# Reordered taps, points, final scaling and rounding in tile 0, an earlier split in tile 1, and four own buffers for the unit turns

## The reference

```python
x = x + _L0_conv_ref(_gn(x), ...)   # depthwise convs, sampled values, attention
x = x + _L1_conv_ref(_gn(x), ...)   # token attention with a wide MLP beside it
```

## Time and profile before

| what | value |
| --- | --- |
| runs | 2822.07, 2825.60, 2829.56 us (median 2825.60) |
| profiled execution, own time | 2823.88 us |
| its span | 2822.1 us |
| TensorE busy | 96% |
| VectorE busy | 70% |
| ScalarE busy | 42% |
| GpSimd busy | 23% |
| mean granted TensorE clock | 0.967 of full |

### The profile page before, as it was taken

The page is one execution under the profiler, slowest core; times in us unless marked ns, Lnnn a source line. Parts: engine busy times, 40 slices in busy tenths (PEclk is TensorE's granted clock), DMA queues, the critical chain, the costliest instruction groups (busy, mean ns, idle before and its releaser), DMA issues.

```text
span 2822.1 us, 40251 instructions
## 1 busy us (share of the span) xinstructions
PE 2697.0 (96%) x14382; PEld 2447.3 (87%) x14382; DVE 1981.0 (70%) x2513; ACT 1176.4 (42%) x2039; POOL 658.5 (23%) x219
## 2 busy tenths in 40 slices
PE   6998799999999999999999999999999999999999
PEld 4556798899998899899998899899999899999998
DVE  5988785888887684988886674888887634434443
ACT  3432465444342465444432265444443254333332
POOL 0020142222222043222224033322224033211220
PEclk9998899999999999999999999999999999999999
DMA  5257632343338632333446743233436832112110
GB/s 222 58 156 258 216 96 81 102 110 113 103 101 255 219 123 82 101 101 101 107 120 200 261 129 100 70 103 110 122 101 178 281 110 79 43 43 52 47 43 30
DMA packets 208431, 347.62 MB, mean 123 GB/s; under 512 B 24288, under 2 KB 191840, under 8 KB 205408
## 3 DMA queue, kind: packets, MB, share of 16 engines
q1 hardware_dynamic: 182192, 311.60, 34.0%
q10 hardware_dynamic: 21552, 14.05, 3.7%
q0 software_dynamic: 4480, 19.27, 2.4%
HBM read 241.31 MB, written 103.56 MB: 122 GB/s over the span
## 4 chain that ended last, share of the span: by engine, by line
PE 71%; issue 10%; DMA 8%; DVE 6%; ACT 3%; POOL 2%; SPq 1%; ACTq 0%; DVEq 0%; POOLq 0%
PE bank L781 15%; PE bank L782 15%; PE bank L783 15%; PE bank L827 3%; PE bank L986 3%; PE bank L988 3%; PE bank L987 3%; PE bank L1177 3%; PE bank L1009 3%; PE bank L1163 2%; DVE AC L2391 2%; DMA r_scr<-rr 2%; POOL rq L701 1%; DMA X<-x_scr 1%; PE bank L1121 1%
## 5 line engine op out<-in xcount | busy, mean ns | idle before, releaser
L1751 ACT ACTIVATE S<-bank,b1p 128x448 f32<-128x448 f32 x336 | 212.4, 632 | 836.6 <-PE bank L783 795.1
L2391 DVE SCALAR_TENSOR_TENSOR AC<-XV,wfold,AC 128x1568 f32<-128x1568 f32 x288 | 530.0, 1846 | 2.8
L781 PE MATMUL bank<-SH,W2H 128*128 128x448 f32 x1008 | 391.3, 388 | 7.8 <-DVE SL L2360 7.7
L781 PE MATMUL bank<-XRH,W1H 128*128 128x448 f32 x1008 | 378.7, 376 | 0.7 <-ACT S L1751 0.7
L783 PE MATMUL bank<-SH,W2L 128*128 128x448 f32 x1008 | 375.9, 373 | 0.0
L782 PE MATMUL bank<-SL,W2H 128*128 128x448 f32 x1008 | 375.7, 373 | 0.0
L782 PE MATMUL bank<-XRL,W1H 128*128 128x448 f32 x1008 | 374.3, 371 | 0.0
L783 PE MATMUL bank<-XRH,W1L 128*128 128x448 f32 x1008 | 372.6, 370 | 0.0
L701 POOL TENSOR_TENSOR rq<-qn,nhalf 112x32 f32<-112x32 f32 x28 | 181.9, 6496 | 465.7 <-DVE qn L2330 465.7
L2360 DVE TENSOR_TENSOR SL<-S,SH 128x448 fp32r<-128x448 f32 x336 | 207.2, 618 | 92.4 <-ACT SH L1754 91.5
L705 POOL TENSOR_TENSOR ro<-on,nhalf 112x32 f32<-112x32 f32 x28 | 180.1, 6434 | 299.5 <-DVE on L2351 299.4
(11 more groups left out here) (228 smaller groups left out, 5171.9 us busy)
## 6 DMA issues: line engine op xcount, KB each, us to landing
XV<-in_xp SPq DMA_DIRECT2D x36, 870.0 KB, 7.3
XC<-in_xp SPq DMA_DIRECT2D x14, 1682.0 KB, 9.9
CQ<-q_scr SPq DMA_DIRECT2D x28, 672.0 KB, 7.1
CX<-in_x SPq DMA_DIRECT2D x28, 672.0 KB, 4.9
x_scr<-CX SPq DMA_DIRECT2D x28, 672.0 KB, 5.3
X<-x_scr SPq DMA_DIRECT2D x28, 672.0 KB, 4.2
V<-v_scr SPq DMA_DIRECT2D x28, 672.0 KB, 7.0
Y<-x_scr SPq DMA_DIRECT2D x28, 672.0 KB
```

Source lines behind the costliest of these rows:

```text
L781: mm(o, wh, xh, start=first, stop=False)
L1751: fn(S[:, j % 2, :], bank[j % 2][:, 0:T], ACT.Silu, bias=b1p[:, j:j + 1]).then_inc(s["s_s"], 1)
L2391: stt(o, XV[h][:, ky:ky + HR, kx:kx + W], wfold[:, kind, k, 3 * ky + kx:3 * ky + kx + 1], o, ALU.mult, ALU.add).then_inc(s["va"], 1)
```

## The change

All edits are in the passes with a next image, in tiles 0 to 3.

- VectorE, tile 0: the taps per place are 0, 1, 1, 1, 2, 2, 2, 2, 2, 2, 1 instead of 0, 0, 0, 1, 2, 2, 2, 2, 2, 2, 3. The first stands before the copy of the offsets, the second before the first `o_scale`. `o_final` moves from behind the sixth split to ahead of the two taps before it; `attended_l` moves ahead of the seventh split; the sixth group of taps moves behind `scale_x` and ahead of `query_norm`. `sampling_points` moves from tile 1 to tile 0, behind the eighth split.
- VectorE, tile 1: the first split stands ahead of the first tap.
- ScalarE, tile 0: `unit_start(0, 0)` stands before `norm_in`; `attended_h` and the tanh stand behind the last `query_out` and ahead of `roots_spread` and `silu(n, 7)`. They stood behind `silu(n, 7)` and at the tile's end.
- Unit turns: groups of 4, 4, 4 and 2 in the same banks 6, 7, 5, 6, with four buffers and four store semaphores instead of three. VT3 lies behind RB, in the room that the sampling stage uses as VS.

(The count of splits starts at 0.)

```diff
+VU = (4, 4, 4, 2)
+VU0 = (0, 4, 8, 12)
...
-        VT2 = sb("VT2", [TS, VG[2] * P], at=at)
-        VT = (VT0, VT1, VT2, VT0)
+        VT2 = sb("VT2", [TS, VU[2] * P], at=at)
...
+        VT3 = sb("VT3", [TS, VU[3] * P], at=[at[0] + T * 4])
+        VT = (VT0, VT1, VT2, VT3)
...
-    VST = (HEAD + 192, HEAD + 112, HEAD + 64)
+    VST = (HEAD + 192, HEAD + 112, HEAD + 64, HEAD)
...
-                    act.wait_ge(s[f"pair_st{i % 3}"], VST[i % 3] + (b * (2 * KC) + c) * (32, 16, 16)[i % 3] + i // 3 * 16)
-                    fn(VT[i][:, 0:VG[i] * P], bank[(6, 7, 5, 6)[i]][0:TS, 0:VG[i] * P], ACT.Copy).then_inc(s["vt_ev"], 1)
+                    act.wait_ge(s[f"pair_st{i}"], VST[i] + (b * (2 * KC) + c) * 16)
+                    fn(VT[i][:, :], bank[(6, 7, 5, 6)[i]][0:TS, 0:VU[i] * P], ACT.Copy).then_inc(s["vt_ev"], 1)
...
                 def tile(n, t):
                     first, last = t == 0, t == STRIPS - 1
                     before = nxt and 1 <= t <= KC
                     silu(n, 0)
                     silu(n, 1)
+                    if nxt and first:
+                        unit_start(0, 0)
                     if not last:
                         norm_in(b * KVX + KVT + t + 1)
                     silu(n, 2)
-                    if nxt and first:
-                        unit_start(0, 0)
                     if before:
                         for i in range(3):
                             unit_out(t - 1, 1, i)
...
                         roots_out(n + 1)
                         query_out(n + 1, 1)
                         query_out(n + 1, 2)
+                        if first:
+                            attended_h(n, first)
+                            if nxt:
+                                tanh(b + 1)
                         roots_spread(n + 1)
                     silu(n, 7)
-                    if not last:
+                    if not first and not last:
                         attended_h(n, first)
                     for j in range(8, JC - 1):
                         silu(n, j)
...
                 alone(act)
                 for t in range(STRIPS - 1):
                     tile(n0 + t, t)
-                    if nxt and t == 0:
-                        tanh(b + 1)
                 if nxt:
                     last_tile(n0 + STRIPS - 1, b + 1)
                 else:
...
                         stt(Y[:, k, :], bank[2 + k][:, 0:T], bo[:, k:k + 1], Y[:, k, :], ALU.add, ALU.add).then_inc(s["y_s"], 1)
 
                 AT = (1, 1, 1, 2, 2, 2, 2, 2, 1, 1, 1)
-                AT0 = (0, 0, 0, 1, 2, 2, 2, 2, 2, 2, 3)
+                AT0 = (0, 1, 1, 1, 2, 2, 2, 2, 2, 2, 1)
 
                 def conv(t, part):
 
...
                     first, last = t == 0, t == STRIPS - 1
                     if not first:
                         output(n - 1)
-                    conv(t, 0)
-                    split_s(n, 0)
+                    if t == 1:
+                        split_s(n, 0)
+                        conv(t, 0)
+                    else:
+                        conv(t, 0)
+                        split_s(n, 0)
                     if nxt and t >= 1:
                         strip_stats(b + 2, t - 1, X0Q)
                     if first:
                         state_heads()
+                        conv(t, 1)
                         if nxt:
                             dve.wait_ge(s["dots"], HEAD + b + 2)
                             cp(OFF[:, :, :].rearrange("p t a -> p (t a)"), bank[7][0:TK, 0:2 * STRIPS]).then_inc(s["off_put"], 1)
                             sampling_offsets(b + 1)
-                    if nxt and t == 1:
-                        sampling_points(b + 1)
-                    conv(t, 1)
+                    if not first:
+                        conv(t, 1)
                     split_s(n, 1)
                     if first:
+                        conv(t, 2)
                         o_scale(n, 0)
                         o_scale(n, 1)
-                    conv(t, 2)
+                    else:
+                        conv(t, 2)
                     if last:
                         o_final(n)
                     else:
...
                         o_norm(n)
                     conv(t, 4)
                     split_s(n, 5)
+                    if first:
+                        o_final(n)
                     conv(t, 5)
                     split_s(n, 6)
-                    if first:
-                        o_final(n)
-                    elif not last:
+                    if not last:
                         attended_l(n)
-                    conv(t, 6)
+                    if not first:
+                        conv(t, 6)
                     split_s(n, 7)
-                    if first:
-                        attended_l(n)
                     if not last:
                         scale_x(n + 1)
+                    if first:
+                        conv(t, 6)
+                    if not last:
                         query_norm(n + 1, 7)
                     conv(t, 7)
                     split_s(n, 8)
+                    if nxt and first:
+                        sampling_points(b + 1)
                     if not last:
                         o_scale(n + 1, 0)
                         o_scale(n + 1, 1)
```

More of the change, by code:

```diff
@@ L201, in build @@
         at[0] = xrr_end
[L202 removed]
+        VT1 = sb("VT1", [TS, VU[1] * P], at=at)
         CQ0 = sb("CQ0", [P, KC, T], at=list(at))
@@ L274, in build @@
             f1 s_s sh sl f2 mh ml pj y_s""".split()
-        names += ["gtp", "oc_ev", "pair_st2"] + [f"gath{t}" for t in range(GR)]
+        names += ["gtp", "oc_ev", "pair_st2", "pair_st3"] + [f"gath{t}" for t in range(GR)]
         s = {n: sem("s_" + n) for n in names}
@@ L290, in build @@
         ahead = """otp ktp oa ka kt_ev kt_st dots off_put va qa vtp vt_ev pair_st0 pair_st1
-            at_mm k_red k_hat v1_st0 v1_st1 k_ev v_ev s_s sl f2 pair_st2 y_s y_st""".split()
+            at_mm k_red k_hat v1_st0 v1_st1 k_ev v_ev s_s sl f2 pair_st2 pair_st3 y_s y_st""".split()
         block = ctx.enter_context(nc.Block())
@@ L553, in store_unit @@
                         c = conv_unit(t, h)
-                        for i in range(len(VG)):
-                            r0 = (h * HT + VG0[i]) * TS
+                        for i in range(len(VU)):
+                            r0 = (h * HT + VU0[i]) * TS
                             sp.wait_ge(s["vt_ev"], VTT + b * (KC * 8) + c * 4 + i + 1)
-                            sp.dma_start(pair_d[r0:r0 + VG[i] * TS, t * P:(t + 1) * P].rearrange("(s p) c -> p s c", p=TS),
-                                         VT[i][:, 0:VG[i] * P].rearrange("p (s c) -> p s c", c=P)).then_inc(s[f"pair_st{i % 3}"], 16)
+                            sp.dma_start(pair_d[r0:r0 + VU[i] * TS, t * P:(t + 1) * P].rearrange("(s p) c -> p s c", p=TS),
+                                         VT[i][:, :].rearrange("p (s c) -> p s c", c=P)).then_inc(s[f"pair_st{i}"], 16)
                     else:
@@ L726, in image @@
                 if nxt:
-                    pool.wait_ge(s["pair_st0"], VST[0] + (b + 1) * (KC * 64))
-                    pool.wait_ge(s["pair_st1"], VST[1] + (b + 1) * (KC * 32))
-                    pool.wait_ge(s["pair_st2"], VST[2] + (b + 1) * (KC * 32))
+                    for i in range(len(VU)):
+                        pool.wait_ge(s[f"pair_st{i}"], VST[i] + (b + 1) * (KC * 32))
                     pool.wait_ge(s["va"], taps_done(b, CV - 1, 0))
@@ L1219, in turn_unit @@
                         pe.wait_ge(s["vt_ev"], VTT + b * (KC * 8) + c * 4 + 1)
-                    for j in range(VG[i]):
-                        last = tr(bank[VTB[i]][0:TS, j * P:(j + 1) * P], AC[h][:, (VG0[i] + j) * TS:(VG0[i] + j + 1) * TS], ident[:, :])
+                    for j in range(VU[i]):
+                        last = tr(bank[VTB[i]][0:TS, j * P:(j + 1) * P], AC[h][:, (VU0[i] + j) * TS:(VU0[i] + j + 1) * TS], ident[:, :])
                     last.then_inc(s["vtp"], 1)
```

2 lines of the change are left out of this document (1 added, 1 removed).

## The result

The changed kernel took 2795.78 us in the median of 6 runs (2790.73 to 2804.53), the kernel before 2823.84: a ratio of 0.9914 [0.989, 0.9938]. One of the six executions of the kernel before took 5983.52 us; it is not in the ratio, and without it the median is 2822.07. So the changed kernel is 26 to 28 us faster by the medians, 0.9% by the ratio; 2815.5 was forecast, with 2808 to 2822 as the range, so the time lies outside it, on the fast side. Measured again, beside the first experiments, it took 2811.83 us (2804.57 to 2818.14, 10 runs) against 2826.08: 0.9946 [0.9927, 0.9964], 14 us. The granted clock of those ten runs was 0.965 to 0.970, that of the first six 0.966 to 0.974. So part of the first gain is clock that these six runs had and the ten had not. Both gains are more than the 8.5 us of my sum: the upper bound of the second interval, 0.9964, is still 10 us.

A forecast was written before the change was run, and what follows sets the result against it. TensorE, busy 2697.0 of 2822.1 us, was taken as the bound. Gains of 3.9 + 8.5 + 4.7 = 17.1 us less 3.5 + 4.2 + 0.9 = 8.6 gave 8.5 us: 2815.5 us forecast, range 2808 to 2822.

The forecast's parts named there:

- my sum: Whole change: removed TensorE waits gain 17.1 us, 8.6 us are given back, leaving 8.5 us.
- The waits named: TensorE's waits: V's 3.4 us and SL's 7.7 go, VT's 5.0 fall to about 0.7, ML's 0.79 stays.
- the two causes given for SL: Tile 1: fewer taps behind the last root and first split ahead of the tap; all five SL waits go, 8.5 us.
- The 0.9 us for X's load: Tile 2's X load shares queues with the output's store: 0.3 us per pass, 0.9 us given back.
- Fourth attend, 3.5 + 3R = 7.7 us given back: Tile 0: the later query root makes TensorE's fourth attend wait 1.1 + R us in each of three passes.
- R: Tile 0: how much later RB's load lands than VectorE wants it; taken as 1.4 us, bounds 0 and 2.5.
- rival (a): Tile 0: RB is as quick as before, R = 0; gain 12.7 us, 2811 us; chance 0.20.
- net nothing, at most 5 us either way: Half clock behind long waits: three such waits removed, three of 2.6 us brought; at most 3 x 1.7 us.
- Rival (d): Clock: half-clock stretches behind long waits cost 1.7 us each, net nothing; no chance of its own given.
- tile 0's order: Tile 0 as a whole loses: 3.9 us gained from V's wait, 7.7 given back at the fourth attend.
- the own buffers: Unit turns: each of six VT waits shrinks by at most 0.8 us, 4.7 us gained in all.
- turned against the change (2819): Idle-gap rule: new, longer waits could each bring a half-clock stretch, 3.4 us more, 2819 us.

The follow-up runs named there:

- the first experiments: The changed kernel again, and with shared buffer, tile 1's order or tile 0's order put back; ratios to the kernel before 0.9946, 0.9978, 0.994, 0.9909.
- the first kernel with spread norms: The changed kernel with the norm products spread, a quarter ahead of fc2(6) and one behind each of its three outputs; 2791.34 us, ratio to before 0.9892.
- the wide base: The changed kernel with norm products spread wider, to the last two thirds of fc1(9), and the fourth attend one step later; 2775.36 us, again 2771.06 (0.9842, 0.9839).

## Why the prediction was wrong

- **The waits named were the right ones.** V 3.4, SL 7.7 and VT 4.4 of 5.0 us went, and ML stayed, as the steps had it. Of the two causes given for SL, the taps were enough; once they are moved, the split ahead of the tap and the points moved out of tile 1 add nothing that the runs show. The 0.9 us for X's load doesn't show either: in tile 1 ScalarE waited 2.23, 0.32 and 0.54 us for it, against 1.54, 1.67 and 1.75 before, and the only wait of TensorE for VT that is left is 0.6 us.
- **Fourth attend, 3.5 + 3R = 7.7 us given back: this term failed too.** The mechanism is right, its size was too large, and the clock hid it. RB was issued 1.5 us after the turn of V began, not 2.2 (489.05 and 487.58), and it had landed when the scaling of X started at 493.95, 4.9 us later:

```profile
489.05 0.35 ACTq L1629 DMA_DIRECT2D RB<-r_scr  x1
```
```profile
493.95 1.56 DVE L2303 TENSOR_TENSOR X<-X,RB 128x1344 f32<-128x1344 f32 x1 [0.29 <-DMA RB<-r_scr]
...
498.95 0.18 DVE L2334 COPY qn<-bank 112x32 f32<-112x32 f32 x1
...
506.24 1.02 DVE L2345 TENSOR_TENSOR QQ<-bank,rq 112x384 f32<-112x384 f32 x2 [0.60 <-POOL rq L704]
```

  VectorE waited 0.29 us for it: R is 0.3, not 1.4, close to the 0 of rival (a), and the wait would have been 1.4 us a pass, 4.4 in all (the first kernel with spread norms shows 1.24, 1.33 and 1.38). V's load was issued at 488.95, just ahead of RB, and landed after 5.8 us, later than RB after 4.9. So RB didn't queue behind V; it took 1.5 us more than the 3.4 of this place before. The Trainium skill, "DMA: Bandwidth & Descriptors", section "Queues, rings and completion order", says that each DMA engine alternates between the queues that have work; the trace agrees, with RB's 4.9 us inside the 3.4 to 6.3 of the earlier trace rows and its landing ahead of V's.
- **The clock, "net nothing, at most 5 us either way": this is the step that failed.** Rival (d) took one fall after one of three waits as chance and looked at no other. Many falls are tied to places, behind the norm block (17 of its 24 places before) and behind long waits, and the change moves them. In its profile the new fall in tile 0 costs 8.5 us and all other half clock is 15.5 us less, so half clock costs 88 us where it cost 95: 7 us gained, not nothing. Of the 25.5 us between the two profiles, 18.5 are left for idle time; 16.2 of them are my gains with X's load taken off and without the attend, 17.1 - 0.9. The single terms point the same way: tile 0's order loses 8.0 us where the sum had 3.8, the own buffers gain 6.6 where it had 4.7, and the taps 11.6 where it had 8.5. Each of these alone is within the spread of the runs from the sum; on the wide base, where the waits are longer too, the taps' 16.7 and the buffers' 12.8 are clear of it. In the second measurement the clock does come to about nothing, with means of 0.967 after and 0.968 before, as (d) had it, but as a balance of larger parts: the 14 us there are near 16.2, with the fall in tile 0 in the place of the attend's wait and about as much clock gained elsewhere. That the forecast was nearer to this measurement is luck in so far as these parts cancel. In the first measurement the mean clock was 0.970, and 0.003 of 2800 us are 8 us more, over half of the 14 by which the two measurements differ.
- **The rule on idle gaps** (the Trainium skill, "TensorE: Matmul & The Clock Gate", section "Why this matters for your kernels", says that idle gaps between bursts of matmuls cost throughput by the clock) was weighed in the prediction for waits alone and turned against the change (2819). Where the waits are several us, the trace agrees (5.41 us idle, 0.54 granted). For the most frequent falls no idle gap is needed: in tile 1 of the kernel before TensorE was busy 3.20 of 3.20 us ahead of the fall. There the measurement decides: the clock fell with no idle gap, behind the block of eight-column products, and in the ten profiles with that block spread it fell behind it in 1 of 240 places.
- **The range** was built from R and the buffers and gave the clock 1.7 us steps; it should have had the run to run spread of the clock (0.965 to 0.970 over ten runs of one kernel, some 14 us) and what the change does to the falls.

Open is why tile 0's block loses the clock in all three passes in one order and in none in the other, with the same instructions and starts a microsecond or so apart: no run changed that start alone. Open is also what set the higher clock of the first six runs, and how much of the 15.5 us of clock gained outside tile 0 is the change's doing: one profile of the kernel before is all there is to compare with, and part of the difference lies in stages that the change doesn't touch.

## What to carry to other kernels

Before the waits of a tuned kernel whose TensorE is busy 96% are summed, list the stretches at half clock and look what stands ahead of each. A block of narrow products that costs 2.4 us by its own time cost up to 3.4 us more behind it, and in the changed kernel spreading it between wide products, with its consumer one step later, gave more than the whole change: from 0.9946 to 0.9842 [0.9814, 0.987] of the kernel before. It is no gain by itself everywhere: in the kernel before, the same edit gave only 0.9959 [0.9945, 0.9973], since a wait on VectorE grew to 5.6 us; the wait and the block had to go together. An instruction moved ahead on an engine that works in order helps its consumer only if what then stands between the two is no longer than before; count both sides of the move.

## What was not expected of the hardware

The clock fell behind 2.4 us of products of 8 columns with TensorE busy throughout, and didn't in any of tiles 1 to 3 above when the same products stood in four groups of six records between outputs of fc2. The same block was followed by 6.7 us of half clock where it started at 493.37, and by none in the kernel where it started at 492.50. Two executions of one program differ by more than 10 us on the same chip (2804.57 and 2818.14, at clocks of 0.969 and 0.967), so a change of this size needs many runs or the trace.
